# A graph network's edge accumulation: VectorE's round loop written out, and the fold of a ring spread between other operations

## What is computed

```python
msg = h[src_a] * norm[:, None]
out = jax.ops.segment_sum(msg, dst_a, num_segments=n)
```

## Time and profile before

| what | value |
|---|---|
| median of 3 runs | 2583.65 us (2583.22 to 2584.04) |
| the profiled execution | 2575.93 us |
| its span | 2574.1 us |
| VectorE busy | 1459.5 us, 57% |
| TensorE matmul busy | 2014.7 us, 78% |
| ScalarE busy | 1053.4 us, 41% |
| GpSimd busy | 921.1 us, 36% |

### The profile page before, as it was taken

How to read it: one execution, slowest core, us unless ns; L and a number is a source line. 1 busy time by engine, 2 the same in 40 slices (tenths; PEclk the granted TensorE clock), 3 DMA queues, 4 the chain that set the end, 5 groups by cost and what they waited for, 6 DMA issues and landing times. The chain is left out here.

```text
span 2574.1 us, 48365 instructions
## 1 busy us (share of the span) xinstructions
PE 2014.7 (78%) x14338; PEld 1700.0 (66%) x14338; DVE 1459.5 (57%) x3333; ACT 1053.4 (41%) x2976; POOL 921.1 (36%) x884
## 2 busy tenths in 40 slices
PE   2888788788599999999989557777777777777772
PEld 1555455455378999999868346676767667667672
DVE  8999899899643111144232445555555555555555
ACT  5899889898522000011121323333333333333330
POOL 0022122212000000000000267777777777777771
PEclk9999999899789999999989555555555555555555
DMA  1456656465768877777646175555555555555541
GB/s 51 61 100 106 95 94 109 80 110 93 136 211 301 289 289 286 295 279 274 211 162 218 42 181 160 156 161 158 157 161 161 161 155 160 159 159 158 161 130 37
DMA packets 226425, 416.22 MB, mean 162 GB/s; under 512 B 131915, under 2 KB 151393, under 8 KB 216545
## 3 DMA queue, kind: packets, MB, share of 16 engines
q1 hardware_dynamic: 187485, 334.92, 46.8%
q0 software_dynamic: 38784, 79.48, 11.7%
HBM read 347.87 MB, written 66.43 MB: 161 GB/s over the span
## 5 line engine op out<-in xcount | busy, mean ns | idle before, releaser
L2225 POOL DMA_INDIRECT attention_windowed_vkv<-kv_dram,ttention_windowed_vsrc x808 | 777.4, 962 | 247.0 <-issue 225.6
L2308 PE MATMUL attention_windowed_vps_s<-attention_windowed_hot,attention_windowed_vmsg 128*104 128x32 f32 x1616 | 322.0, 363 | 270.1 <-DVE attention_windowed_vmsg L2365 268.4
L646 ACT ACTIVATE add_edges_hot_lo<-add_edges_hot_lo,add_edges_parts 128x128 bf16<-128x128 bf16 x1616 | 488.2, 387 | 66.9 <-DVE add_edges_hot_lo L754 66.4
L2308 PEld LDWEIGHTS attention_windowed_vps_s<-attention_windowed_hot,attention_windowed_vmsg 128*104 128x104 f32 x1616 | 295.1, 288 | 311.2 <-DVE attention_windowed_vmsg L2365 250.7
L684 PE MATMUL add_edges_ps_pair<-add_edges_hot,add_edges_hot_lo 128*128 128x300 bf16 x2424 | 450.0, 296 | 0.0
L2296 PE MATMUL attention_windowed_vps_e<-attention_windowed_vwe,attention_windowed_vattr 97*128 97x96 f32 x1616 | 404.2, 432 | 24.6 <-ACT attention_windowed_hot_T L2253 24.6
L1219 PE MATMUL graph_layers_acc<-graph_layers_w_tab,graph_layers_g 125*96 125x125 f32 x3750 | 417.7, 269 | 0.0
L1219 PEld LDWEIGHTS graph_layers_acc<-graph_layers_w_tab,graph_layers_g 125*96 125x96 f32 x3750 | 406.6, 163 | 0.0
L2296 PEld LDWEIGHTS attention_windowed_vps_e<-attention_windowed_vwe,attention_windowed_vattr 97*128 97x128 f32 x1616 | 368.8, 333 | 25.5 <-issue 25.4
L678 PE MATMUL add_edges_ps_pair<-add_edges_hot,add_edges_hot_lo 128*128 128x300 bf16 x808 | 241.6, 299 | 129.1 <-DVE add_edges_strip L785 84.5
L785 DVE TENSOR_TENSOR add_edges_strip<-add_edges_strip,add_edges_ps_pair 128x600 f32 x404 | 311.4, 771 | 17.3 <-PE add_edges_ps_pair L684 13.6
(11 more groups left out here) (233 smaller groups left out, 2159.3 us busy)
## 6 DMA issues: line engine op xcount, KB each, us to landing
graph_layers_w_tab<-w_blocks SPq DMA_DIRECT2D x75, 1562.5 KB
graph_layers_c_tab<-c_blocks SPq DMA_DIRECT2D x75, 800.0 KB
w_blocks<-add_edges_strip SPq DMA_DIRECT2D x25, 1562.5 KB, 16.4
attention_windowed_vattr<-in_attr_T SPq DMA_DIRECT2D x202, 192.0 KB
attention_windowed_vdrow<-dstf_dram SPq DMA_DIRECT2D x202, 192.0 KB
c_blocks<-add_edges_counts SPq DMA_DIRECT2D x25, 800.0 KB, 14.5
attention_windowed_vkv<-kv_dram,ttention_windowed_vsrc POOLq DMA_INDIRECT x808
ttention_windowed_q_rows<-q_dram SPq DMA_DIRECT2D x202, 18.0 KB
```

The costliest lines, as they stand in the source:

```text
L646: done = nc.scalar.activation(hot_lo[s][:, 1 + part, j, :], hot_lo[s][:, 0, j, :], ACT.Copy, scale=parts[:, part, bass.ds(g * G + j, 1)])
L2225: nc.gpsimd.indirect_dma_start(out=kv[s][:, k, :], out_offset=None, in_=kv_dram, in_offset=bass.IndirectOffsetOnAxis(ap=src4[s][:, k:k + 1 ...
L2308: last = nc.tensor.matmul(ps_s[s % 2][:], msg[s][:, k, :], hot[s][:, k, :], start=k == 0, stop=k == Q4 - 1)
```

## The change

Two edits, both for VectorE in `add_edges`. `rounds` gets a flag, and VectorE's call sets it: rounds 1 to 25 are then all written out with constants in place of registers; ScalarE and TensorE keep the loop. And in a round with a fold, the order becomes lanes, first add, tiles, third, fold, second add, first half of places, clearing of the 12 columns, finish, third add, and the rest as before. In the other rounds the order stays.

```diff
-        def rounds(eng, body):
+        def rounds(eng, body, written_out=False):
 
             body(0, 0, range(2, 4))
+            if written_out:
+                for r in range(1, LAST_ROUND):
+                    body(r, r % SLOTS_B, range(4))
+                body(LAST_ROUND, LAST_ROUND % SLOTS_B, range(NG - (4 * LAST_ROUND - 2)))
+                return
...
                     closes = k == 0 and reaches(r, 2)
+                    folds = closes and rm == 2
                     if more:
                         lanes(g + 1, s)
-                    if closes:
+                    if closes and not folds:
                         dve.wait_ge(added, 4 * g)
-                        if rm == 2:
-                            fold(r)
-                        else:
-                            finish(r, rm)
-                    if closes and more:
+                        finish(r, rm)
+                        if more:
+                            tiles(g + 1, s)
+                        dve.wait_ge(block_done, r - 1)
+                    add(4 * g, 0, at[0])
+                    if more and (folds or not closes):
                         tiles(g + 1, s)
-                    if closes and rm == 2:
-                        if more:
-                            third(g + 1, s)
+                    if more:
+                        third(g + 1, s)
+                    if folds:
+                        dve.wait_ge(added, 4 * g + 1)
+                        fold(r)
                         dve.wait_ge(folded, 2 * ((r - 2) // SLOTS_B) + 1)
+                    add(4 * g + 1, 1, at[1])
+                    if more:
+                        places(g + 1, s, 0)
+                    if folds:
+                        dve.wait_ge(added, 4 * g + 2)
                         nc.vector.memset(strip[:, :, :, RING:RING + WINDOW], 0.0).then_inc(folded, 1)
                         finish(r, rm)
                         dve.wait_ge(folded, 2 * ((r - 2) // SLOTS_B) + 2)
-                    if closes:
                         dve.wait_ge(block_done, r - 1)
-                    add(4 * g, 0, at[0])
-                    if more and not closes:
-                        tiles(g + 1, s)
-                    if more and not (closes and rm == 2):
-                        third(g + 1, s)
-                    add(4 * g + 1, 1, at[1])
-                    if more:
-                        places(g + 1, s, 0)
                     add(4 * g + 2, 2, at[2])
...
-            rounds(dve, body)
+            rounds(dve, body, written_out=True)
```

## The result

The changed kernel takes 2551.74 us (median of 4 runs, 2550.31 to 2552.12) against 2583.43 us for the kernel before in the same comparison: a ratio of 0.9876, 95% interval 0.9859 to 0.9894. The forecast was 2552.1 us. The profiled execution's own time is 2550.31 us, its span 2546.2.

The account below looks back on a forecast made before the run. VectorE, busy 22.80 of 22.80 us in a written-out round, was taken to bound the accumulation. Round 1 (22.64), ordinary rounds (387.6) and fold rounds (148.8) gave 559.0 against 590.6; 2583.65 - 31.5 = 2552.1 us, 8-in-10 range 2545 to 2564.

Parts of the forecast that it names:

- The bound: In the accumulation's loop stretch VectorE limits: each idle microsecond costs the kernel one; ScalarE is 0.9 us per round behind.
- the ring: Time from VectorE's start of round 1 to round 25: 590.6 us before, forecast 559.0 after.
- Edit 1: Writing out VectorE's loop removes idle before `lanes` and late adds: 23.6 us by waits, ordinary rounds at 22.80 us.
- Edit 2: Spreading the fold in six fold rounds: from 155.7 us together to 148.8, 6.9 us less.
- I expect no fall from these, and no add waits for TensorE: In new fold rounds TensorE stands about 1.3 us twice, not 3.25 once; its clock stays full.
- The self waits: VectorE's waits on its own last result in a fold round: two, before second and third add, 0.22 us each.
- What is late next: In fold rounds `finish` comes some 5.2 us after `lanes`, against 2.8, delaying ScalarE's conversion, SyncE's store and the clearing.
- The clearing chain: Weights' store, 15.4 us, then GpSimd's clearing, 2.73 us, hold VectorE's next register load about 0.15 us per fold round.
- The sum: Round 1, 17 ordinary rounds and six fold rounds of 24.8 us total 559.0 us, saving 31.5 us.
- The clearing rival: Store lands 1.0 to 1.5 us later, each fold round grows: 6 to 9 us, 2558 to 2561; chance 0.12.
- Fetch pauses in straight code: Written-out VectorE rounds bring four or five pauses, 16 to 20 us: 2568 to 2572; chance 0.06.
- ScalarE's pause at its turn: ScalarE's 3.3 us loop pause, now uncovered five times, could cancel the gain: about 2580 us; chance 0.04.

Follow-up runs that it names:

- e1: VectorE's rounds written out, fold order as before the change, against the kernel before: 2559.01 us against 2579.78, ratio 0.9918.
- e3: Changed kernel with VectorE's rounds 5 to 20 in a loop of two turns of eight rounds: 2558.38 us; kernel before 2579.28.
- e4: Changed kernel with ScalarE's and TensorE's rounds written out too: 2551.8 us; kernel before 2579.78, ratio 0.9899.
- e6: Changed kernel with GpSimd clearing half of the weights' slot once more before the full clearing: 2564.23 us; kernel before 2579.28.
- e7: Changed kernel unaltered, run again on another chip beside the kernel before: 2867.81 us against 2890.89, ratio 0.9903.
- e2: VectorE's loop kept and only the fold spread, against the kernel before: 2572.68 us against 2579.78, ratio 0.9976.
- e5: Changed kernel with fold ahead of third and finish ahead of the 12 columns' clearing: 2551.55 us; kernel before 2579.78.

## Why the prediction was right, and where it was lucky

**The bound.** Right. Every microsecond that VectorE no longer idles came out of the phase: the next phase's first VectorE operation starts at 654.98 us instead of 683.48, 28.5 us earlier. That is the 29.56 of the ring, less 0.55 before round 1 and 0.5 behind round 25.

**Edit 1.** Right in size and in place. Taking today's fold rounds (155.7 us) with ordinary rounds at 22.80, the working gives 590.6 - 22.64 - 387.6 - 155.7 = 24.7 us; e1 measured 24.45. That it's a pause per branch back and a smaller gap per looped start is shown by e3. What the pause goes with can be read in the trace of the kernel before. Its DMA records mark the packets that carry instructions. From VectorE's branch at 256.3 to its next instruction at 259.2 one such packet is all that the core's DMA engines move (256.4 to 259.2; the last line is queue and kind: packets, MB, share of the engines):

```profile
DMA packets 1, 0.01 MB, mean 3 GB/s; under 512 B 0, under 2 KB 0, under 8 KB 0
...
q14 instruction: 1, 0.01, 1.0%
```

So it is at the other three turns: one instruction packet in each of the windows 356.9 to 359.7, 456.8 to 459.7 and 558.3 to 561.1. At its own branch in the same loop TensorE goes on after 0.3 us, with no packet between:

```profile
L580 PEldq COMPARE_BRANCH  x1: 224/224/224, 254.9 to 254.9; - x1
...
L580 PEldq FUSED_REGOPS  x1: 83/83/83, 255.2 to 255.2; - x1
```

So the long pause is not the price of every branch back; it comes with an instruction fetch, as the Trainium skill's rule ("Runtime: NRT & Kernel Launch", section "Instruction fetch mechanics") has it. How much of the 2.8 us is the fetch itself stays open: the packet begins some 1.0 us behind the branch, and VectorE goes on some 1.4 us after it has landed.

**Edit 2.** Right in sign, too large in size. The forecast was 6.9 us; alone it measured 4.88, and on top of edit 1 it gave 566.13 - 561.02 = 5.11. The step that failed is "I expect no fall from these, and no add waits for TensorE". The clock did fall behind two pauses of 1.26 and 1.11 us (1.20 in round 2) in three of six fold rounds, and adds then waited 0.59, 0.53 and 0.57 us. Those three rounds last 0.72 to 0.82 us more than round 14, which has neither a fall nor a late start behind it (24.55 us, against the 24.65 worked out). Six rounds of 24.55 us, 2.3 us for the falls and 0.98 us for late starts make the 150.58 us measured, where 148.8 were forecast. The step rested on one round: round 6 is the only fold round of the kernel before in which the clock stayed at 1.00. Behind the pauses of 2.76 to 3.25 us in the other five it fell to 0.50, which the prediction's own trace showed. With the new order the count varies from trace to trace: none of six in e3, two in e4 and e6, three in the changed kernel and e7, five in e2. The self waits were taken at 0.22 us each and measured 0.21, where the Trainium skill's rule ("VectorE: DVE Perf Modes", section "The DRAIN you can't avoid") had nothing; the row decided rightly.

**What is late next.** The clearing chain was put at 0.15 us late in every fold round. It measured 0.82 us once, 0.16 once, and nothing in round 14 and in the three rounds that TensorE had already made longer: 0.98 us against the 0.9 forecast for all six, right in total and not in its spread. The store took 16.1 us in the one long case, and not 15.4; in the other five fold rounds it took 15.1 to 15.5. e6 shows the mechanism, e5 its removal. ScalarE's conversion waited for `finish` 13.2 us in six times, 2.2 each, as worked out, and no operation of VectorE waited for ScalarE from 60 to 650 us.

**The sum.** The ring was forecast at 559.0 us and measured 561.02, or 31.5 us saved against 29.56. The forecast time hit within 0.4 us nevertheless, and that is partly luck. The step from the profiled execution to the median, "7.7 us above that execution, and I expect the same", didn't hold: the changed kernel's median is 1.4 us above its profiled execution. Against the profiled executions alone, 2544.4 was forecast and 2550.31 measured. Of those 25.62 us, the ring gives 29.56, the stretches either side of it take 1.05 back, the later phases 0.6, and the time outside the span 2.3 (4.1 instead of 1.8 us). The last two lie within what executions of one kernel differ by.

**Rivals.** The clearing rival is real as a mechanism, but worth 1 us, not 6 to 9. Fetch pauses in straight code: one idle of 0.35 us at the start of round 9 in each of the versions with VectorE all written out, its cause not found, and none of 2.8 us, over 20 rounds. ScalarE's pause at its turn stays covered, shown by e4.

## What to carry to other kernels

Look at the idle time before the first operation of a loop's turn on the engine that bounds the phase. If its queue is kept short by semaphores, the branch and the register loads are paid in full there, while an engine with work queued hides the same pause (ScalarE here: 0.3 us of idle over all its turns), so write out the bounding engine's program alone. Spread rare extra work between the operations that cover it, but then check what hangs on its last step: here a store and a clearing moved from slack to the edge. And measure a 1% effect in the stretch where it happens; whole executions of the kernel before varied by 10 us, twice what edit 2 is worth.

## What the runs showed of the hardware

Two pauses of TensorE of 1.26 and 1.11 us, 1.24 us of work between them, were followed by the half clock in some rounds and not in others of the same execution; in the kernel before, one pause of 3.24 us was not, and four of 3.25 us were. The length of the pause alone doesn't decide it here, and what does was not found.

The same program took 2868 us on one chip and 2552 on another, with equal ring times (560.91 and 561.02 us). Most of the difference lies in the attention phase: from its first gather to its last it takes 1323.1 us there and 1023.2 here, 300 of the 325 us between the two spans. Between 1600 and 2000 us from the span's start, GpSimd issues 241 operations there and 317 here, at nearly the same time each (972 and 961 ns for a gather, mean from 1800 to 2200 us). These two rows are of that stretch, the changed kernel on the first chip and then e7, columns as in the earlier trace rows:

```profile
1600.00:2000.00 400.00, 293.89 (x1588) 278.29 (x1588) 221.08 (x554) 134.69 (x316) 303.63 (x317) 0.50 0.57 159
```

```profile
1600.00:2000.00 400.00, 220.24 (x1199) 209.85 (x1199) 166.32 (x420) 102.38 (x240) 233.29 (x241) 0.50 0.44 121
```

GpSimd waits there for VectorE's messages (90.5 of these 400 us, against 11.3). VectorE's waits in front of L2360 and L2380 come to 372 us from 1700 to 2400, 282.5 of them put down to something outside the core; on the first chip they come to 278, none of them put down to that and 197.2 to the gather's DMA. The cause was not found.
